# Transformer block on one core: output projection of the third batch moved beside the last batch's row maxima, a later last turn, later rounding of the second weights, values and output exchanged

## The reference

```python
h = layernorm(x)
Q, K, V = (h @ W.T + b for each of Wq, Wk, Wv)   # heads of 16 columns
attn = softmax(Q @ K.T / sqrt(16))               # 512 x 512 for each of 16 heads
x = x + (attn @ V) @ Wo.T + bo
x = x + ffn(layernorm(x))                        # W1, W3, silu, Walsh-Hadamard, W2
x = x + memory(layernorm(x))                     # gates, decaying sum along the sequence
x = x + ffn(layernorm(x))
```

## Time and profile before

| | us |
|---|---|
| median of 3 runs (564.72 to 565.11) | 565.0 |
| the profiled execution, its own time | 566.53 |
| its span | 564.7 |
| PE busy in the span | 552.5 (98%) |
| DVE busy | 382.9 (68%) |
| ACT busy | 311.8 (55%) |
| POOL busy | 178.4 (32%) |

### The profile page before, as it was taken

One profiled execution on the slowest core, in us unless ns is written; L12 is line 12 of the kernel. 1 busy time (PEld: TensorE's weight loads), 2 busy tenths in 40 slices (PEclk: granted clock), 3 DMA queues, 4 the chain that ended last, 5 costly groups with the idle time before them and its releaser, 6 DMA issues.

```text
span 564.7 us, 8930 instructions
## 1 busy us (share of the span) xinstructions
PE 552.5 (98%) x3220; PEld 383.0 (68%) x3220; DVE 382.9 (68%) x729; ACT 311.8 (55%) x581; POOL 178.4 (32%) x209
## 2 busy tenths in 40 slices
PE   8999999999999998999999999999999999999997
PEld 4543343344434433468888888888888888988887
DVE  6988888898898899836465545746886437363333
ACT  3668889876987797743233223366775333323231
POOL 5794467562546242520202002233332010100100
PEclk9989999999999999999999999999999999999999
DMA  7354540231023030021001020110000210112101
GB/s 231 100 180 146 168 132 3 68 128 34 3 94 133 6 147 3 2 74 25 15 7 31 1 38 2 21 18 1 0 2 1 37 39 15 23 38 38 38 1 37
DMA packets 48443, 29.41 MB, mean 52 GB/s; under 512 B 33496, under 2 KB 41688, under 8 KB 48016
## 3 DMA queue, kind: packets, MB, share of 16 engines
q1 hardware_dynamic: 47180, 27.77, 17.1%
q10 hardware_dynamic: 1220, 1.07, 0.7%
HBM read 10.89 MB, written 5.24 MB: 29 GB/s over the span
## 4 chain that ended last, share of the span: by engine, by line
PE 91%; DVE 4%; ACT 2%; issue 1%; DMA 1%; ACTq 0%; POOL 0%; SPq 0%; POOLq 0%
PE PS L392 89%; DVE mxr L1096 2%; PE PS L403 1%; ACT PR L921 1%; PE PS L590 1%; DMA ring<-mT 1%; DMA X<-in_x 1%; DVE OT L1161 0%; ACTq L883 0%; DVE X L1265 0%; DVE X L1178 0%; ACTq L907 0%; DVE bst L1050 0%; PE PS L527 0%; POOL rstd L1338 0%
## 5 line engine op out<-in xcount | busy, mean ns | idle before, releaser
L392 PE MATMUL PS<-xTh,ring 128*128 128x512 f32 x608 | 188.1, 391 | 0.0
L1096 DVE TENSOR_REDUCE mxr<-PS 128x1 f32<-128x512 f32 x256 | 162.9, 680 | 25.5 <-PE PS L392 24.6
L921 ACT ACTIVATE PR<-PS 128x512 f32<-128x512 f32 x256 | 138.0, 602 | 30.3 <-PE PS L392 29.9
L392 PEld LDWEIGHTS PS<-xTh,ring 128*128 128x128 f32 x608 | 113.2, 188 | 23.7 <-issue 1.7
L392 PE MATMUL PS<-xTl,ring 128*128 128x512 f32 x304 | 110.1, 391 | 0.0
L793 ACT ACTIVATE AOh<-PR 128x512 fp32r<-128x512 f32 x72 | 45.5, 632 | 111.4 <-DVE PR L1235 105.9
L392 PE MATMUL PS<-ring 50*128 50x512 f32 (+1 forms) x512 | 100.0, 454 | 4.4 <-DVE mxr L1096 2.8
L1342 POOL TENSOR_TENSOR xTl<-xf,xTh 128x512 fp32r<-128x512 f32 x30 | 42.4, 1428 | 164.9 <-ACT xTh L793 164.9
L1235 DVE TENSOR_TENSOR PR<-PR,PS 128x512 f32<-128x512 f32 x64 | 43.4, 678 | 71.9 <-PE PS L392 51.8
L392 PEld LDWEIGHTS PS<-ring 50*128 50x128 f32 (+1 forms) x512 | 41.6, 185 | 71.1 <-ACT PR L921 43.2
L1088 DVE TENSOR_TENSOR AOl<-PR,AOh 128x512 fp32r<-128x512 f32 x72 | 51.0, 709 | 45.5 <-ACT AOh L793 45.4
(11 more groups left out here) (134 smaller groups left out, 623.6 us busy)
## 6 DMA issues: line engine op xcount, KB each, us to landing
ring<-qh SPq DMA_DIRECT2D x48, 128.0 KB, 2.8
xf<-PR SPq DMA_DIRECT2D x112, 32.0 KB, 1.9
ring<-ql SPq DMA_DIRECT2D x24, 128.0 KB, 2.8
ring<-weight_scratch SPq DMA_DIRECT2D x3, 1024.0 KB, 4.8
weight_scratch<-in_w SPq DMA_DIRECT2D x2, 1024.0 KB, 6.8
X<-in_x SPq DMA_DIRECT2D x3, 512.0 KB, 4.7
out<-X SPq DMA_DIRECT2D x6, 256.0 KB, 2.2
X<-in_w SPq DMA_DIRECT2D x1, 1024.0 KB, 5.5
```

The costliest lines, as they stand in the source:

```text
L392: return nc.tensor.matmul(dst, lhsT, rhs, start=start, stop=stop, skip_group_check=True)
L921: nc.scalar.activation(PR[:, j % 8, :], PS[:, kq_bank(j), :], ACT.Exp, scale=HD ** -0.5)\
L1096: nc.vector.tensor_reduce(mxr[:, S % 2, blk, TT * p + t:TT * p + t + 1], PS[:, QK0 + i % 3, :], AX.X, ALU.max, negate=True).then_inc(max_d ...
```

## The change

- The output projection of batch 2, in batch 3, moves from steps 20 and 24, 26 to steps 8, 10 and 12, 14 (`LAST_OUT_AT`), and the two additions to X from steps 21 and 27 to steps 11 and 15.
- In batches 1 and 2 the second half of the values' projection and the second half of the output projection change places: values at 24, 26, output at 28, 30. What each waits for changes with it, and so does what the turns wait for.
- The last turn of maxima (group 15) moves from step 19 to step 20 on PE, ACT and SP. POOL's split of it stays at step 19.
- ACT makes the high part of the first half of the output at step 31 in batches 0 to 2 (28 before), and at step 21 in batch 3.
- POOL makes the matching low part at step 5 of the next batch (29 of its own before), and at step 22 in batch 3.
- DVE rounds the second weights in steps 26 to 29 (23 to 26 before).

```diff
-OUT_AT = ((20,), (24, 26))
-V_AT = ((22,), (28, 30))
-
-MAX_AT = 3
+OUT_AT = ((20,), (28, 30))
+V_AT = ((22,), (24, 26))
+
+LAST_OUT_AT = ((8, 10), (12, 14))
+
+MAX_AT, LAST_MAX_AT = 3, 20
+
+AO_AT, LAST_AO_AT = STEPS - 1, 21
...
+        def out_at(b):
+            return LAST_OUT_AT if b == BATCH - 1 else OUT_AT
+
+        def turned_at(K):
+
+            S = (K + LEAD) // 8 - 1
+            if S == LAST_GROUP - 1:
+                return S if K % STEPS == LAST_MAX_AT else None
+            return S if K % 8 == MAX_AT and S < LAST_GROUP else None
...
# PE, turn_maxima
-                elif s // 8 < 3 and b < BATCH - 1:
+                elif b == BATCH - 1:
+                    pe.wait_ge(x_done, 2 * b - 2 + s // 8)
+                elif s // 8 < 3:
                     pe.wait_ge(qk_f, 4 * b + 2 * (s // 8))
-                elif s // 8 == 3:
-                    pe.wait_ge(*((x_done, 2 * b) if b else (w2h_done, 3)))
+                else:
+                    pe.wait_ge(*((v_copied, 2 * b + 4) if b else (w2h_done, 3)))
...
# PE, shared_bank
-                    pe.wait_ge(*((v_copied, 2 * b + 2) if b > 1 else (w2h_done, 4)))
+                    pe.wait_ge(*((x_done, 2 * b - 2) if b > 1 else (w2h_done, 4)))
                     ln_transpose(0, MB)
...
-                if s == OUT_AT[0][0] and b:
-                    pe.wait_ge(aol_done, 2 * b)
-                    pe.wait_ge(mt_ready, turned)
-                    for part in range(2):
-                        out_projection(0, part)
-                if s in OUT_AT[1] and b:
-                    if s == OUT_AT[1][0]:
-                        pe.wait_ge(*((v_copied, 2 * b + 3) if more else (x_done, 2 * b - 1)))
-                    out_projection(1, OUT_AT[1].index(s))
+                for half in range(2):
+                    at = out_at(b)[half]
+                    if b and s in at:
+                        if s == at[0]:
+                            pe.wait_ge(aol_done, 2 * b)
+                            pe.wait_ge(mt_ready, turned)
+                        for part in range(2) if len(at) == 1 else (at.index(s),):
+                            out_projection(half, part)
...
                 if b and s in V_AT[1] and more:
                     if s == V_AT[1][0]:
-                        pe.wait_ge(mt_ready, turned)
+                        pe.wait_ge(v_copied, 2 * b + 3)
...
# ACT
-                if s == OUT_AT[1][-1] + 2:
+                if s == (LAST_AO_AT if b == BATCH - 1 else AO_AT):
                     act.wait_ge(aof_ready, 2 * b + 1)
...
# DVE
-                            if s == OUT_AT[half][-1] + 1:
+                            if s == out_at(b)[half][-1] + 1:
                                 add_attention(b - 1, half)
...
-                if b == BATCH - 1 and SPLIT_AT <= s < SPLIT_AT + 8:
-
-                    w_split_hi((s - SPLIT_AT) // 4, (s - SPLIT_AT) % 4)
+                if b == BATCH - 1:
+
+                    for w, at in ((W_UP, SPLIT_AT), (W_LIN, 26)):
+                        if at <= s < at + 4:
+                            w_split_hi(w, s - at)
...
# POOL
+                if s == 5 and b:
+                    output_lo(2 * b - 1)
                 if s == 6 and b:
                     output_lo(2 * b)
-                if s == OUT_AT[1][-1] + 3:
+                if s == LAST_AO_AT + 1 and b == BATCH - 1:
                     output_lo(2 * b + 1)
```

More of the change, by code:

```diff
@@ L352, in _ @@
                         weights_in(W_LIN)
[L353 to L356, removed]
+                    S = turned_at(STEPS * b + s)
+                    if S is not None:
+                        max_rows(S)
                     if b == 0 and s == 24:
@@ L659, in _ @@
                     weigh_values((K - 3) // 2)
-                S = (K + LEAD) // 8 - 1
-                if s % 8 == MAX_AT and S < LAST_GROUP:
+                S = turned_at(K)
+                if S is not None:
                     turn_maxima(S, b, s)
@@ L962, in _ @@
                             qk_split(b + 1, n)
-                if s % 8 == MAX_AT and (K + LEAD) // 8 - 1 < LAST_GROUP:
-                    max_evacuate((K + LEAD) // 8 - 1)
+                S = turned_at(K)
+                if S is not None:
+                    max_evacuate(S)
             act.wait_ge(aof_ready, 2 * BATCH)
```

## The result

| | before | after |
|---|---|---|
| median of 4 runs, us | 564.86 (564.48 to 565.11) | 574.88 (574.50 to 575.56) |
| the profiled execution | 566.53 | 574.75 |
| its span | 564.7 | 572.9 |
| its mean granted clock | 0.997 | 0.988 |

The change makes the kernel slower: the medians differ by 10.0 us. The ratio on record is 1.0167, with a 95% interval of 1.0139 to 1.0195 (the medians alone give 1.0177). The forecast had the direction right (569.4, 4.4 us more than before) and the size wrong; 574.88 lies 3.2 us above the end of its range.

What follows compares the result with a forecast made beforehand. Bound: PE, but a DVE-PE loop in steps 4 to 18 of batch 3. Sum 3.6 + 2.0 - 0.5 + 1.8 + 0.1 - 3.3 + 0.7 = +4.4, so 569.4 us against the median; range 567.2 to 571.7.

Steps and rivals of the forecast that it cites:

- Part 1: Step 4, batches 1 to 3: DVE's transpose back waits for POOL's late low part, stalling PE: +3.6 and +2.0 us.
- (a): Rival: POOL finishes the late low part before DVE needs it at step 4, so no wait: 563.1 us; chance 0.07.
- (c): Rival: the stalls cost half, 2.8 instead of 5.6, and no clock fall: 565.9 us; chance 0.05.
- Part 2: Values and output exchanged in batches 1 and 2: step 27's turn no longer waits for DVE's addition, -0.5 us.
- Part 3: Projection in steps 8 to 15 of batch 3: those take 7.02 and 6.47 us, +1.8; late second addition +0.1.
- Part 4: Steps 19 to 31 of batch 3: without the projection ACT's exponentials bound, last weighing earlier, -3.3 us, at most -3.5.
- (d): Rival: the maxima's rows land late for step 24 and the tail gains only 2.3: 570.4 us; chance 0.10.
- Part 5: TensorE's clock: a fall to half speed costs 1.5 us; half of one fall taken after the stalls, +0.7.
- (b): Rival: each of the three stalls brings a clock fall, 3.7 + 4.5 = +8.2: 573.2 us; chance 0.13.

Runs made afterwards that it cites:

- the early low part: The kernel after, with POOL's late low part of the output made at step 0 of the next batch instead of step 5: 563.47 us, ratio 0.9982.
- the turn's experiment: The kernel after with that low part at step 0, and the last turn of maxima back at step 19 instead of 20: 564.66 us, ratio 0.9998.
- the projection in quarters: The kernel after with that low part at step 0, and the projection's second half in four pieces at steps 12, 14, 16, 18: 564.45 us, ratio 0.9987.
- the late low part alone: The kernel before, with only POOL's low part of the output's first half moved to step 5 of the next batch: 576.9 us, ratio 1.0162.
- the shorter wait: The kernel after, with POOL's low part at step 4 instead of 5, ahead of the placing of values: 567.57 us, ratio 1.0025.

## Why the prediction was right in direction and wrong in size

- **Part 1 was right**, in mechanism, place and price. DVE waited 1.9 to 2.3 us at step 4 of three batches, PE stood still for 1.5 to 1.9, batch 2 lost 1.8 as worked out, and the three waits together cost 5.6, the sum's own number. Rivals (a) and (c), an empty wait or half a wait, are out.
- **Part 2 was right at the turns and too high in sum**: -0.70 in the trace of after for -0.5, and the wait for X at step 27 is gone. But the exchange alone gives about 0.3 back at steps 0 to 11 of the next batches, and was worth 0.2 in time.
- **Part 3 was right**: 7.01 and 6.48 against 7.02 and 6.47, and 0.12 behind them.
- **Part 4 had the right path and too small a gain**: -3.85 against -3.3, and beyond its own bound, "at most -3.5". Two of its reasons were wrong. "DVE rounds the second weights from 233.5 to 238 ... so nothing" looked at when the rounding must be done, and not at what it stands in front of: left at step 23 it holds back the transpose of the output. At full clock the projection alone is 0.5 slower than before, where the early low part without the exchange's 0.2 would be some 1.9 faster; of these 2.4 the turn is 1.0 and some 1.4 are left for the roundings. And the later turn was argued through PE's wait for POOL. The sum, which goes by ACT's order with the turn behind step 20, held its gain without saying so; the expectation of the turn's experiment then put it at nothing. It is worth 1.0, since ACT was the engine that waited for it. Rival (d) did not come about: the maxima's rows held PE for 0.15 us in step 24 of the kernel with the early low part and about as long in after, and the tail gained 3.8 all the same. The margin is thin: with the projection in quarters they held PE for 0.54.
- **Part 5 failed**, and with it the number. The step was "I take half of one fall ... +0.7". The price of a fall was sized well (1.5; the rows have 1.6 and 1.6). The count was wrong. The standstills of batches 1 and 3 each brought one in after's profiled execution, 3.1 together, and in the late low part alone batch 2's and batch 3's did. My reason against it, that the work around the stall is dense in batches 1 and 2, was disproved by both. Rival (b), 573.2, had this mechanism, and I gave it 0.13.
- **A second fault of part 5** was in the comparison with the median. The profiled execution of before holds the fall near 40 us and its other runs mostly don't. By subtracting 1.5 I took for granted that after would be as free of it. In after's profiled execution that fall lasts twice as long and costs 3.0 of the 6.6 us; this half of the miss has nothing to do with the standstills. Whether the four runs of after have it by chance or because of the change isn't settled: nothing that the change touches comes ahead of it, and the kernel with the early low part shows it in some executions and not in others.

Without the clock the sum was 3.7, and 3.4 was measured. So the terms for the engines' waits held, their errors partly offset each other, and the term for the clock was 0.7 where 3.1 fell behind the standstills and 3.0 near the start. The warning about idle gaps that the prediction quoted from the Trainium skill ("TensorE: Matmul & The Clock Gate", section "Why this matters for your kernels") concerns gaps longer than these; by it there would have been no fall, and the runs contradict that use of it: standstills of 1.9, 1.7, 1.55 and 1.17 us each went with half a clock, though others of the same length (1.51 in batch 2 of after) did not.

## What to carry to other kernels

When a step is moved on a slow in-order engine, look for every wait on its counter, and ask whether the waiter now comes before it: here one low part, 1.3 us of an engine busy for 31% of the span, held DVE, its maxima and PE in a row. Then look at what stands behind the moved step on its own engine, even if nobody is in a hurry for its result. And a standstill of TensorE has two prices, its length and the half clock that may follow; if the wait can't be taken away, a few products of no use in it bring back the second. Here the waits cost 5.6 and the falls behind them 3.1 in after's profiled execution.

## What was not expected of the hardware

- The clock fell in or up to 2 us behind standstills of 1.2 to 1.9 us, behind some and not behind others of the same kernel, and stayed at 0.50 for some 3.4 us (batches 1 and 3 of after) to some 10 (batch 3 of the late low part alone and of the shorter wait). In after PE was busy without a gap during it.
- The same kernel before took 564.5 to 575 us on the same chip, and nearly all of that spread goes with the granted clock (1.000 down to 0.978). Small changes could be read only from executions at full clock.
- DVE's cast of a 128x512 tile of weights took 0.36 to 0.42 us while POOL did no low part, and 1.0 on average beside POOL's low parts (four in a row in the projection alone); its own low part took 0.69 and 1.65. That POOL is the cause is argued from the times, not tested. That is how a rounding that looked like 4 us of slack work came to block a transpose.
